# Scores of two fp32r parts on 32 rows a head instead of three bf16 parts on 64, with the row maxima regrouped

## The reference

```python
# branch 1 (16 heads of 8): attention weights 1 - tanh(energy)^2, causal
pressure = einsum('bhid,bhjd->bhij', q, k) * scale
pressure = where(causal, -10000.0, pressure)
energy = (pressure - phase_threshold) / tau
attn = 1 - tanh(energy)**2; attn /= sum(attn) + 1e-6
s = (attn @ v) @ Wo.T
# branch 2 (16 heads of 8): RMS norm, softmax attention, RMS norm, experts
attn = softmax(q @ k.T * scale); X = xn + (attn @ v) @ wo
h2 = rmsnorm(X); combine = softmax of the best two of 8 router logits
out = X + swiglu_shared(h2) + sum over experts of combine * swiglu_e(h2)
result = x + s * silu(out)
```

## Time and profile before

| what | value |
|---|---|
| median of three runs | 1154.11 us |
| profiled execution, own time | 1157.05 us |
| its span (first to last instruction) | 1155.2 us |
| TensorE matmul, busy | 1032.3 us (89%) |
| TensorE weight load, busy | 471.8 us (41%) |
| VectorE, busy | 856.3 us (74%) |
| ScalarE, busy | 652.9 us (57%) |
| GpSimd, busy | 347.4 us (30%) |
| mean granted TensorE clock | 0.97 of full speed |

### The profile page before, as it was taken

How to read it: one execution, slowest core, us unless ns; L and a number is a source line. 1 busy time by engine, 2 the same in 40 slices (tenths; PEclk the granted TensorE clock), 3 DMA queues, 4 the chain that set the end, 5 groups by cost and what they waited for, 6 DMA issues and landing times.

```text
span 1155.2 us, 18598 instructions
## 1 busy us (share of the span) xinstructions
PE 1032.3 (89%) x6912; PEld 471.8 (41%) x6912; DVE 856.3 (74%) x1716; ACT 652.9 (57%) x888; POOL 347.4 (30%) x194
## 2 busy tenths in 40 slices
PE   3459999989999999999999899999999889999998
PEld 1102355324652346423554245522465235542364
DVE  7447687759977597786877589775986869774872
ACT  4027862588326972378624884269723786248831
POOL 6500335103630154303352035400552033520023
PEclk9558999999999999999999999999999999999999
DMA  5540225103441045201251024310342113500020
GB/s 176 117 54 2 49 68 132 34 2 77 109 68 29 3 96 127 38 20 44 64 141 25 11 63 122 69 28 2 96 116 41 30 29 69 148 9 20 1 75 9
DMA packets 71785, 69.65 MB, mean 60 GB/s; under 512 B 8528, under 2 KB 63056, under 8 KB 71568
## 3 DMA queue, kind: packets, MB, share of 16 engines
q1 hardware_dynamic: 68928, 64.41, 24.7%
q10 hardware_dynamic: 2768, 4.06, 1.0%
HBM read 53.37 MB, written 14.81 MB: 59 GB/s over the span
## 4 chain that ended last, share of the span: by engine, by line
PE 56%; DVE 21%; ACT 11%; DMA 4%; issue 3%; SPq 3%; POOL 1%; ACTq 0%; DVEq 0%; POOLq 0%
PE O L1019 9%; PE O L1035 8%; DVE nmax L677 7%; DVE PT L714 7%; ACT PT L554 6%; PE S L1051 6%; PE S L1053 5%; PE S L994 5%; PE S L1052 5%; PE M L963 4%; PE M L960 4%; PE M L946 2%; DVE PT L840 2%; SPq L337 2%; SPq L327 1%
## 5 line engine op out<-in xcount | busy, mean ns | idle before, releaser
L554 ACT ACTIVATE PT<-S 128x1024 f32<-128x1024 f32 (+1 forms) x448 | 420.7, 971 | 117.3 <-PE S L994 115.0
L677 DVE TENSOR_REDUCE nmax<-M 128x1 f32<-128x512 f32 x512 | 330.6, 685 | 119.4 <-PE M L960 80.4
L714 DVE SCALAR_TENSOR_TENSOR PT<-PT 128x768 f32<-128x768 f32 (+1 forms) x192 | 215.6, 1171 | 96.4 <-ACT PT L554 96.0
L1019 PE MATMUL O<-PT,V 128*12 128x256 f32 (+3 forms) x2816 | 242.2, 424 | 0.0
L423 POOL TENSOR_TENSOR split<-split,parts 128x512 f32<-128x512 f32 x32 | 91.0, 2844 | 433.2 <-ACT parts L514 433.2
L438 POOL TENSOR_TENSOR PT<-PT,CB 128x1024 f32<-128x1024 f32 x56 | 133.2, 2385 | 278.0 <-DMA CB<-scrC 158.2
L588 ACT ACTIVATE PT<-S 128x1024 f32<-128x1024 f32 x72 | 73.9, 1027 | 250.7 <-PE S L1053 250.6
L994 PE MATMUL S<-stackQ,stackK 64*128 64x512 bf16 (+3 forms) x1024 | 192.1, 347 | 21.6 <-DMA stackQ<-mTZ 8.4
L1051 PE MATMUL S<-h2hi,wgu_hi 128*128 128x512 f32 x288 | 150.5, 522 | 0.1
L1035 PE MATMUL O<-PT,wdn 128*128 128x512 f32 x288 | 142.7, 595 | 0.0
L960 PE MATMUL M<-KX,stackQ 128*128 128x512 bf16 x256 | 104.3, 409 | 28.5 <-DMA KX<-scrK 21.3
(11 more groups left out here) (189 smaller groups left out, 1042.5 us busy)
## 6 DMA issues: line engine op xcount, KB each, us to landing
CB<-scrC SPq DMA_DIRECT2D x64, 256.0 KB, 5.7
stackQ<-scrQ SPq DMA_DIRECT2D x192, 64.0 KB
stackK<-scrK SPq DMA_DIRECT2D x192, 64.0 KB
scrQ<-parts SPq DMA_DIRECT2D x16, 384.0 KB, 5.0
scrK<-parts SPq DMA_DIRECT2D x16, 384.0 KB, 7.8
KX<-scrK SPq DMA_DIRECT2D x96, 32.0 KB
PT<-in_w_gu ACTq DMA_DIRECT2D x2, 1152.0 KB, 8.0
xin<-in_x SPq DMA_DIRECT2D x8, 256.0 KB, 2.9
```

What stands on the lines that cost most here:

```text
L554: a.activation(PT[:, n % SLOTS, 2 * q * w:2 * q * w + 2 * w].rearrange("p (r n) -> p r n", r=2), S[k][:, :].rearrange("p (r n) -> p r n", ...
L677: v.tensor_reduce(nmax[:, h % 2, h // 2, t:t + 1], M[k][:, :], AX.X, ALU.max, negate=True).then_inc(m_read[k], 1)
L714: v.scalar_tensor_tensor(p, p, 1.0, p, ALU.subtract, ALU.mult).then_inc(weighed, 1)
L1019: last = t_.matmul(O[k][32 * q:32 * q + VW, i0:i1], V[:, j, 4 * g + q, :], PT[:, n % SLOTS, w * q + at:w * q + at + i1 - i0], start=(j == ...
```

## The change

1. Two parts instead of three, in fp32r instead of bf16: three pairs of parts (0,0), (0,1), (1,0) stand on 24 of 32 rows, and four heads share the 128 rows. The stacks hold the same number of bytes, KX has four slots of three groups instead of two of four. ScalarE writes the first part in fp32r; GpSimd makes the second in one step.
2. Row tiles: the scores of half a unit use two of four 32-row tiles; a maximum of the units 0 to 8 is issued right behind the scores of a half and uses one of the other two tiles (slots 2, 3 beside half 0, slots 0, 1 beside half 1).
3. Eight of Y's sixteen maxima move to experts 7 and 8 of the row before (four each), where they use the zero-padded KX, and X and W move up: the experts 1 to 8 hold 3, 5, 5, 5, 6, 6, 6, 4 maxima where they held 0, 5, 4, 4, 5, 6, 6, 2. The units 0 to 8 hold 2, 2, 4, 3, 3, 3, 3, 2, 2 where they held 1, 3, 4, 4, 4, 3, 4, 4, 5.
4. The rows of a run of maxima go in four DMAs of two rows each; parts of the maxima and their transposes are fp32r.
5. Less scratch for dynamic DMA descriptors makes room.

```diff
-PAIRS = [(0, 0), (0, 1), (0, 2), (1, 0), (1, 1), (2, 0)]
-HP = H // 2
-HALF = 64
+PAIRS = [(0, 0), (0, 1), (1, 0)]
+PARTS = 2
+SLOT = 32
...
-spread(MAX["Y"], {0: 1, 1: 3, 2: 4, 3: 4, 4: 4})
-spread(MAX["Z"], {5: 3, 6: 4, 7: 4, 8: 5})
-PLACES[3].insert(2, "outT")
-PLACES[5].insert(2, "maxT_Y")
+spread("Y", {EXPERT + 7 + e: n for e, n in enumerate((4, 4))})
+EARLY = list(MAX["Y"])
+spread_beside("Y", {0: (1, 1), 1: (1, 1), 2: (2, 2)})
+spread_beside("Z", {3: (1, 2), 4: (2, 1), 5: (1, 2), 6: (2, 1), 7: (1, 1), 8: (1, 1)})
+PLACES[3].insert(1, "outT")
+PLACES[4].insert(2, "maxT_Y")
...
-spread(MAX["X"], {EXPERT + e: n for e, n in enumerate((0, 0, 5, 4, 4, 3))})
-spread(MAX["W"], {EXPERT + 5 + e: n for e, n in enumerate((2, 6, 6, 2))})
+spread("X", {EXPERT + e: n for e, n in enumerate((0, 3, 5, 5, 3))})
+spread("W", {EXPERT + 4 + e: n for e, n in enumerate((2, 6, 6, 2))})
+PLACES[EXPERT + 7] = PLACES[EXPERT + 7][4:] + PLACES[EXPERT + 7][:4]
...
-        parts = [sb(f"parts{i}", [128, 3, L], bf16) for i in range(2)]
-        stack = {n: sb("stack" + n, [128, HP, L], bf16) for n in ("Q2", "K2", "Q1", "K1")}
-        KX = sb("KX", [128, 2, PADDED, L], bf16)
+        parts = [sb(f"parts{i}", [128, PARTS, L], fp32r) for i in range(2)]
+        stack = {n: sb("stack" + n, [128, NG, L], fp32r) for n in ("Q2", "K2", "Q1", "K1")}
+        KX = sb("KX", [128, 4, PADDED, L], fp32r)
...
-                g.tensor_tensor(s[:, :], s[:, :], p[:, 0, :], ALU.subtract).then_inc(pool_step, 1)
-                g.tensor_tensor(p[:, 1, :], s[:, :], ones[:, 0:1].broadcast_to([128, L]), ALU.mult).then_inc(pool_step, 1)
-                g.tensor_tensor(p[:, 2, :], s[:, :], p[:, 1, :], ALU.subtract).then_inc(parts_ready, 1)
+                g.tensor_tensor(parts[i][:, 1, :], split[i][:, :], parts[i][:, 0, :], ALU.subtract).then_inc(parts_ready, 1)
...
             def maximum(u, name):
+                rows = slice(SLOT * i, SLOT * i + ROW_ADD)
+                t_.matmul(M[k][:, :], stack["Q2"][rows, g, t * 128:t * 128 + 128], stack["K2"][rows, g, :],
                           start=True, stop=True).then_inc(m_full[k], 1)
...
             def scores(it, n, q):
-                        rows = slice(HALF * r, HALF * r + HALF)
+                        rows = slice(SLOT * (2 * q + r), SLOT * (2 * q + r) + SLOT)
...
+                    if n < N1:
+                        for q, part in enumerate((names[:u.cut[n]], names[u.cut[n]:])):
+                            scores(it, n, q)
+                            for name in part:
+                                if name[0] == "max":
+                                    work(u, it, name)
+                            if n in v_at and v_at[n] % NT > 0:
+                                with_v(it, v_at[n], q)
+                            elif n in v_at and q == 0:
+                                with_v(it, v_at[n])
+                            for name in part:
+                                if name[0] != "max":
+                                    work(u, it, name)
+                        continue
```

More of the change, by code:

```diff
@@ L105, in __init__ @@
         self.places = {n: [w for w in work if here.get(w, following if w in AHEAD else own)] for n, work in PLACES.items()}
+        self.cut = {n: sum(w not in HALF1 for w in work) if n < N1 else len(work) // 2 for n, work in self.places.items()}
         self.order = [w for n in sorted(self.places) for w in self.places[n]]
@@ L229, in program @@
                   .rearrange("p (e n) -> p e n", e=NE) for i in range(2)]
-        scratch = {n: nc.dram_tensor("scr" + n, [3, 128, L], bf16).ap() for n in stack}
+        scratch = {n: nc.dram_tensor("scr" + n, [PARTS, 128, L], fp32).ap() for n in stack}
         weights_of = nc.dram_tensor("scrC", [E, L], fp32).ap()
@@ L564, in row @@
                     weights(it, n, 0)
-                    for name in names[:len(names) // 2]:
+                    for name in names[:u.cut[n]]:
                         take(u, name, bt)
@@ L571, in row @@
                         acc_out(it, outs[n])
-                    for name in names[len(names) // 2:]:
+                    for name in names[u.cut[n]:]:
                         take(u, name, bt)
@@ L682, in maxima_parts @@
                     dve.wait_ge(*read(u, b))
-                p0, p1 = RUNS[run]
-                src = nmax[:, :, p0:p1, :].rearrange("p r h t -> p r (h t)")
-                hi, lo = (dst[:, part, :].rearrange("p (r n) -> p r n", r=2) for part in range(2))
+                src = nmax[:, :, RUNS[run], :]
+                hi, lo = (dst[:, :].rearrange("p (i a t) -> p a i t", i=4, a=PARTS)[:, part] for part in range(PARTS))
                 step(v.tensor_copy(hi, src))
@@ L915, in _ @@
                 maxima_parts(FIRST, run)
+            for name in EARLY:
+                maximum(FIRST, name)
             for it in range(B):
@@ L1147, in first_scores, with second_scores @@
                     scores(it, 0, q)
+            def second_scores(u, it):
+                for q, part in enumerate((u.places[0][:u.cut[0]], u.places[0][u.cut[0]:])):
+                    scores(it, 1, q)
+                    for name in part:
+                        work(u, it, name)
             def row(u, it, following):
@@ L1155, in row @@
                         pe.wait_ge(setup, 2)
-                    for run, (p0, _p1) in RUNS.items():
-                        if n == NT * (p0 // 2) and n:
+                    for run, g in RUNS.items():
+                        if n == NT * g:
                             pe.wait_ge(row_in[run], (it + 1) * 64)
@@ L1187, in row @@
                     work(u, it, "maxT_W")
-                    for q in range(2):
-                        scores(it + 1, 1, q)
-                    for name in ROWS[it + 1].places[0]:
-                        work(ROWS[it + 1], it + 1, name)
+                    second_scores(ROWS[it + 1], it + 1)
                 for t in range(NT):
@@ L1207, in _ @@
             first_scores(0)
-            for q in range(2):
-                scores(0, 1, q)
-            for name in ROWS[0].places[0]:
-                work(ROWS[0], 0, name)
+            second_scores(ROWS[0], 0)
             for it in range(B):
```

148 lines of the change are left out of this document (73 added, 75 removed).

## The result

The changed kernel takes 1266.9 us (median of 4 runs, 1257.99 to 1277.97) against 1154.29 of the kernel before, run on the same chip: ratio 1.0958, 95% interval 1.0884 to 1.1032. The forecast was 1130, with 1100 to 1160 as its range, and none of its cases reaches 1267. The execution profiled is the longest of the four, 1277.97 us with a span of 1276.1; the steps are compared with it as with the 1157.05 of before, so they show some 11 us more than the median, 1.4 a row. Runs over 1.5% longer than the fastest of their kernel, here the profiled one, count as slow and are left out of every ratio and interval, which is why a ratio need not be the quotient of two medians. The other three have a mean granted clock of 0.878 to 0.892, against 0.874 in the profiled one and 0.970 before, so what follows on the clock is not peculiar to the longest.

A forecast was written before the change was run, and what follows sets the result against it. No one engine was taken to rule: VectorE, ScalarE or TensorE bound different stretches, with the chain mostly TensorE's. Seven rows -14.7, last row -2.3, start -7: 1157.05 - 24.0 - 2.9 = 1130 us, range 1100 to 1160.

The forecast's parts named there:

- Step 1: Softmax units 2 to 8: nine maxima fewer, the rest beside scores on free row tiles; 21.2 to 16.6 us, -4.6 a row.
- A and B: Row stretches: A, softmax units 2 to 8, 21.2 us, forecast -4.6; B, units 9 to 15, 15.8 us, forecast +0.4.
- the rival of the queue: Weight loads of the row tiles queue up, each 0.11 us after the last: +5.5 a row, about 1190 us; chance 0.10.
- Step 2: TensorE's score groups: fp32r weights load slower than bf16, charged 0.10 us per half unit, bounds 0 and 0.19.
- C: First half of the sigmoid units, 18.8 us, with GpSimd's splitting of Q2 and K2 inside; forecast -1.2 a row.
- D: Second half of the sigmoid units, 16.9 us, TensorE on the path; forecast +1.0 a row, 0 to 1.6.
- Step 3: First half of the sigmoid units: GpSimd splitting from three passes to one; VectorE gains 2.3 us or 1.1, taken as -1.2.
- Step 4: Experts: eight maxima more, 0.23 us each on TensorE; +2.0 and +0.6 us a row, ends 1.9 and 5.2 in all.
- E and F: The experts, two stretches of a row, 54.9 us together; forecast +2.0 for E and +0.6 for F.
- The rival that named this size: Experts and sigmoid units take it back: full VectorE pays eight maxima at 0.646 us, +5.2; 1161 us; chance 0.17.
- Step 5: Kernel start: two GpSimd passes fewer and half as many load pieces bring first scores earlier; -7 us, 0 to -9.
- G: Border to the next row: fewer maxima in unit 1 let unit 2's scores go earlier; -0.3 us, 0 to -0.7.

The follow-up runs named there:

- 32-row filler: Changed kernel plus an extra, overwritten matmul of 512 bf16 columns on one 32-row tile ahead of every half softmax unit's scores: 1259.09 us, ratio 1.0841.
- old order: Changed kernel with TensorE's earlier order in the softmax units, maxima after the scores among the pieces of the product with V: 1301.61 us, ratio 1.1287.
- eight fillers a row: Changed kernel plus an overwritten 128-row matmul of 512 bf16 columns ahead of each half's scores in units 0 to 3 only: 1218.49 us, ratio 1.0577.
- regrouped kernel before: Kernel before (three bf16 parts, 64 rows a head) with only the maxima moved, 40 among the experts and 24 in the softmax units: 1175.38 us, ratio 1.0212.

## Why the prediction was wrong

**Step 1 failed, in the sentence "So in A TensorE needs 14 x 0.98 = 13.7 ... thus 16.6".** All its prices were read at a granted clock of 1.00, and the sum held them there. The runs in which A stands at both clocks in one kernel give 8.6 us (32-row filler), 10.7 (old order) and, in bf16, where the fall is shorter, 4.8 (32 rows, twice) and 7.3 (64 rows). In the changed kernel A and B together are 46.5 and, with the clock held by eight fillers a row, 36.6 of which four fillers of 0.2 are not its own: the clock costs 10 to 11 us in A and B, more than the 9.5 that they lost and most of the 14.7 of a row. No rival spoke of the clock.

Just before the fall in the row shown TensorE had been busy 7.33 of the 8.18 us of units 1 and 2 (536.79 to 544.97), and 6.65 of 7.74 in the regrouped kernel before (497.43 to 505.17), where the clock stays: at this grain idle time does not tell the two apart. Why the clock falls stays open; the runs say what goes with it. Operand type tells most (bf16 on the same tiles: no fall in three of rows 1 to 6, 17 us in the others), filled rows some, the work in the first units decides. How much type and height weigh by themselves was not settled: fp32r on 64-row tiles, whose stacks take twice the space, was not tried. The Trainium skill, TensorE: Matmul & The Clock Gate, section "What's actually happening", lets the clock fall when TensorE idles. This trace shows it at 1.2 GHz for 24 us of a stretch with TensorE busy 27.00 of 27.30, and here the measurement decides.

Without the clock, Step 1 would still have missed. At full clock A is 18.3 (regrouping only), 18.5 (bf16 beside the scores) or 20.0 - 0.8 = 19.2 (fp32r, four fillers taken off), never 16.6. Three readings in it were off.
- It took 29 maxima from the trace of A and 20 from the lists. The same stretch holds 22 in every full row of the regrouped traces, since some of unit 1's are read in it, so VectorE loses seven and not nine: it is busy 14.74 in A of the regrouped kernel before, not 13.4.
- The 0.31 of a lone maximum is not what every maximum cost. In the kernel before 13 of the 27 recorded in A already start with a score on the other 64 rows (491.85 and 491.86 above), so free row tiles had far less to save than Step 1 counted. In the changed kernel it is 14 of 20, in the changed kernel with eight fillers 11.
- TensorE was to need 14.3. With the eight fillers it is busy 18.74 of the 20.0 (four fillers and the matmuls' tails included). In the bf16 row of 18.5 it waits 1.5 us, in four places, for an M buffer that VectorE has to free, which the worse end of the range had named; what sets the rest was not taken apart.

The tiles did run side by side, as Step 1 had it and against the rival of the queue. Four weight loads, two of them for maxima:

```profile
536.59 0.18 PEld L970 LDWEIGHTS M<-stackK,stackQ 24*128 24x128 f32 x1 [0.24 <-ACT mTW L501]
536.60 0.18 PEld L1001 LDWEIGHTS S<-stackQ,stackK 32*128 32x128 f32 x1
536.60 0.18 PEld L970 LDWEIGHTS M<-stackK,stackQ 24*128 24x128 f32 x1
536.70 0.18 PEld L1001 LDWEIGHTS S<-stackQ,stackK 32*128 32x128 f32 x1
```

Three start within 0.01 us; the fourth is 0.1 behind. As just said, two tiles at once was nothing new.

**Step 2 was about right.** The loads last 0.18 at full clock. B at full clock is 16.6, +0.8 (forecast +0.4); C is 18.8 in fp32r and 17.4 in bf16, so twelve groups cost 1.4 (1.2 was set against C's gain); D +0.3 to +0.5 (forecast +1.0).

**Step 3 was right in kind and too large.** In the run that does only that VectorE gains 1.7 in C (16.34 to 14.64), between the 1.1 and the 2.3 of the forecast, and C 1.4. It is just what the fp32r loads take, so C came out at 0 and not at -1.2.

**Step 4 failed by its place, not its price.** "E +2.0, F +0.6" is in sum what the eight maxima cost without the knot (2.5 measured in the kernel before); the change puts three at expert 1, and E and F cost 5.8. The rival that named this size blamed a full VectorE; it is busy 23.27 of 29.3 in E, less full than before. The sentence on E priced busy time and left out what stands behind a maximum on TensorE.

**Step 5 failed in the clause "if the stores, a third bigger, don't eat it".** First scores are 2.1 us later, not 7 earlier. SyncE's queue after:

```profile
29.09 4.07 SPq L345 DMA_DIRECT2D KX<-scrK  x12
...
37.39 0.39 SPq L338 DMA_DIRECT2D scrQ<-parts  x1
37.82 0.47 SPq L338 DMA_DIRECT2D scrK<-parts  x1
55.34 4.07 SPq L350 DMA_DIRECT2D stackQ<-scrQ  x12
```

and with bf16:

```profile
24.61 4.08 SPq L345 DMA_DIRECT2D KX<-scrK  x12
...
32.92 0.39 SPq L338 DMA_DIRECT2D scrQ<-parts  x1
33.35 0.47 SPq L338 DMA_DIRECT2D scrK<-parts  x1
35.11 4.07 SPq L350 DMA_DIRECT2D stackQ<-scrQ  x12
```

With one pass KX's loads do go out earlier, at 29.09 against 31.87 before. But the first maximum can start only at 44.44, 15.4 later; before it started at 42.25, 10.4 later, and in bf16 it starts at 30.21, 5.6 behind 24.61. Q1's stores take until 55.34 against 35.11. The number of DMAs, which the forecast counted, is the same; the bytes are not: a DMA into KX carries 48 KB where it carried 32, a store 512 KB where it was 384. Then 40 maxima at half clock go at 0.79 each, where 0.646 was counted.

**G** was a little better than forecast (-0.9 for -0.3).

## What to carry to other kernels

A price read at full clock holds only if the changed work keeps the clock: where operands or tiles of a stretch change type or height, put the clock's fall beside the rivals and price it from rows at both levels (here A at 20.7 and 29.3 us). Where work is moved between instructions that hand buffers to each other, follow whose buffer the first moved instruction needs and what the engine that frees it does just before; busy shares do not show a knot. A filler that holds the clock in one stretch has to be judged over the whole row, since the fall can come back in a later one. The better half of this change, 40 maxima among the experts, placed clear of expert 1, is worth 0.8% without fp32r.

## What had not been expected of the hardware

- TensorE's clock fell to 1.2 GHz in a stretch in which it was busy 27.00 of 27.30 us, in every row, and stayed at 2.4 GHz there with eight more 512-column matmuls on 128 rows (0.2 us each) in units 0 to 3, four ahead of the stretch and four in it. It then fell among the experts, for 3.4 to 10.2 us a row.
- fp32r and bf16 instructions of equal shape and order differ in this: with bf16 the fall came in three of six rows and was 17 us long instead of 31.
- At the start, where both run at 1.2 GHz, maxima on all 128 rows go at 0.79 us each in fp32r and 0.70 in bf16 (a pair every 1.58 and 1.39 us).
- A matmul on 48 rows starts within 0.02 us of one on the other 64 rows; one on 24 rows does not run beside one on 64 (none of 20 within 0.3 us), though it does beside those on 32 (14 of 20 within 0.02).
